# A two-layer transformer with experts: the small attention's end inside the next score loop, query/key products earlier between rows, other groups and another tail

## The reference

```python
x = _layernorm(x + _L0_attn_ref(x, ...))   # rms norm, 16 heads of 64, softmax over 256 keys
x = _layernorm(x + _L0_ffn_ref(x, ...))    # shared expert + 8 experts of 256, gates of the top 2
x = _layernorm(x + _L1_attn_ref(x, ...))   # per token: softmax over its own 16 heads of 8
x = _layernorm(x + _L1_ffn_ref(x, ...))    # 8 experts of 512, a token goes through its top 2
```

```python
scores = jnp.einsum('bnhd,bngd->bnhg', q, k) / SCALE
attn = jax.nn.softmax(scores, axis=-1)
out = jnp.einsum('bnhg,bngd->bnhd', attn, v)
```

## Time and profile before

| | us |
|---|---|
| median of 3 runs | 1618.16 (1617.31 to 1619.76) |
| the profiled execution | 1612.05 |
| its span, first to last instruction | 1610.3 |
| from the first to the last `OUT` residual (15 periods) | 1332.46 |
| behind the last `OUT` residual | 217.59 |
| granted TensorE clock, mean | 0.909 |

### The profile page before, as it was taken

How to read it: one execution, slowest core, us unless ns; L and a number is a source line. 1 busy time by engine, 2 the same in 40 slices (tenths; PEclk the granted TensorE clock), 3 DMA queues, 4 the chain that set the end, 5 groups by cost and what they waited for, 6 DMA issues and landing times. The chain is left out here.

```text
span 1610.3 us, 30931 instructions
## 1 busy us (share of the span) xinstructions
PE 1291.1 (80%) x10473; PEld 1110.6 (69%) x10473; DVE 983.1 (61%) x2660; ACT 776.3 (48%) x2206; POOL 626.6 (39%) x550
## 2 busy tenths in 40 slices
PE   6887878787888898898977888898888888876543
PEld 5776667675767787777766676786767676766533
DVE  4466666666566766767666655666775666644612
ACT  5664645455456555555544544465555444422110
POOL 3034352526162524243452624425163442533322
PEclk9998998898799999999998888999998899887756
DMA  7301211010021110201112120111032040115452
GB/s 245 122 2 51 78 44 60 1 50 1 11 89 60 50 57 20 79 14 41 60 54 68 54 65 12 59 49 40 23 115 89 11 133 12 63 41 185 141 165 64
DMA packets 79711, 103.76 MB, mean 64 GB/s; under 512 B 10042, under 2 KB 46531, under 8 KB 79555
## 3 DMA queue, kind: packets, MB, share of 16 engines
q1 hardware_dynamic: 75458, 93.38, 17.5%
...
...
## 5 line engine op out<-in xcount | busy, mean ns | idle before, releaser
L805 ACT ACTIVATE probs<-bank_S,neg_max 128x256 f32<-128x256 f32 x512 | 236.3, 477 | 227.8 <-DVE neg_max L922 204.7
L922 DVE TENSOR_REDUCE neg_max<-bank_S 128x2 f32<-128x512 f32 x256 | 164.7, 685 | 85.3 <-PE bank_S L1378 79.8
L683 POOL TENSOR_TENSOR hid<-hid,qkv 128x1024 f32<-128x1024 f32 x62 | 174.3, 2812 | 32.7 <-ACT hid L821 32.6
L1484 PE MATMUL bank_F<-down,hid 128*128 128x128 f32 x1024 | 136.6, 293 | 39.3 <-DVE x L1004 24.8
L638 POOL TENSOR_TENSOR var_eps<-mv,ln_eps 128x2 f32<-128x2 f32 x64 | 12.7, 198 | 398.0 <-DVE mv L960 397.9
L698 POOL DMA_INDIRECT xs<-x,slots_of x64 | 63.4, 990 | 257.7 <-DVE slots_of L1109 243.1
L1484 PEld LDWEIGHTS bank_F<-down,hid 128*128 128x128 f32 x1024 | 128.8, 206 | 46.2 <-DVE x L1004 29.4
L784 ACT ACTIVATE probsT<-bank_T 128x512 f32<-128x512 f32 x256 | 142.0, 609 | 34.4 <-PE bank_T L1407 31.8
L1407 PE MATMUL bank_T<-ident,probs 128*128 128x128 f32 x1024 | 150.8, 293 | 0.2 <-ACT probs L805 0.2
L671 POOL TENSOR_TENSOR hid<-qkv 128x1024 f32<-128x1024 f32 x47 | 115.6, 2460 | 76.0 <-ACT qkv L784 76.0
L1407 PEld LDWEIGHTS bank_T<-ident,probs 128*128 128x128 f32 x1024 | 122.2, 151 | 31.4 <-issue 29.3
...
## 6 DMA issues: line engine op xcount, KB each, us to landing
...
```

Of the source, the lines that this page charges most:

```text
L683: ins = g.tensor_tensor(pv1[:, t, half(i)], *weights_and_values(t, i), ALU.mult)
L805: ins = sc.activation(probs[:, h // 2 % 2, h % 2, t, :], unit.bank(f"S{h}")[:, t * S:(t + 1) * S], ACT.Exp, bias=neg_max[:, h, t:t + 1], a ...
L922: ve.tensor_reduce(neg_max[:, h, :], v.bank(f"S{h}")[:, :].rearrange("p (t k) -> p t k", t=NT), AX.X, ALU.max, negate=True).then_inc(max_r ...
L1484: ins = te.matmul(bank[:, (j * NT + t) * P:(j * NT + t + 1) * P], hid0[:, e, k, tokens(t)], down0[:, e, k, :], start=k == 0, stop=k == M0 - 1)
```

## The change

The arithmetic stays the same; order, buffers and grouping change.

- **The small attention's end.** `AOT`, `PROJ`, `X3T` and `R1` leave the seam. They stand in the score loop of the next iteration: `AOT` at step 0, `PROJ` at step 1, `X3T` and `R1` at step 4, `RK` at (5, 1), that is behind `T10` and `T11` and ahead of the scores `S14` and `S15`. `route(1)` (now `second_route`) runs on DVE in step 5 behind `head_scores(0)`, `place_row` in step 6, `gate` and `gate_row` in step 7, `map_blocks` behind that. `scatter` stands behind `value_product(0)` on POOL.
- **The seam.** `QK0` and `QK1` come ahead of `X1T`, `S0` and `S1` behind `U0_3`. DVE's `first_pair(0)` comes ahead of `ln_apply(0)`, `first_pair(1)` behind `X1T`, the first maxima behind `route(0)`. A wave that opens a group stands at the seam's end, other waves partly ahead of `X1T`.
- **Buffers.** `x3T`, `score1` and the second half of the products (`prod1`) get their own.
- **Groups.** Rows go in groups of 3, 4, 4, 4 and 1 in place of 4, 4, 4, 3 and 1. Waves have at most 6 blocks and begin at iterations 4, 8 and 12. Seven rows are gathered in the loop in place of eight; `combine` stands at step 3 and its norm at step 7. The last row's blocks are packed without gaps. The number of blocks, 99, stays.
- **The tail** has an order of its own (`tail_first`, `tail_second`): 12 blocks in iteration 16 and 22 in iteration 17, in place of 19 and 11.

```diff
-SLOTS = 8
+GROUPS = [range(0, 3), range(3, 7), range(7, 11), range(11, 15), range(15, 16)]
+COMPACT = len(GROUPS) - 1
+SLOTS = 6
 X3_ROWS = 10
...
-WAVE_SIZES = [(0, 5, [6, 6, 6, 5]), (1, 9, [6, 6, 6, 5]), (2, 13, [8, 8, 7])]
+WAVE_SIZES = [(0, 4, [5, 5, 5, 4]), (1, 8, [6, 6, 6, 5]), (2, 12, [6, 6, 6, 5])]
 WAVES = [(g, sum(sizes[:i]), n, first + i, first + i + 1) for g, first, sizes in WAVE_SIZES for i, n in enumerate(sizes)]
-WAVES += [(3, 0, 8, 16, 16), (3, 8, 8, 16, 16), (3, 16, 3, 16, 16), (4, 0, 8, 17, 17), (4, 8, 3, 17, 17)]
-
-GATHERS = {9: [0, 1], 10: [2, 3], 13: [4, 5], 14: [6, 7]}
+WAVES += [(3, 0, 6, 16, 16), (3, 6, 6, 16, 16), (3, 12, 6, 17, 17), (3, 18, 5, 17, 17), (4, 0, 6, 17, 17), (4, 6, 5, 17, 17)]
+
+GATHERS = {8: [0, 1], 9: [2], 12: [3, 4], 13: [5, 6]}
...
-FILL_B = {(0, 1): ["D0p2"], (1, 0): ["WT0"], (1, 1): ["D0p3"], (2, 0): ["D0base"], (3, 0): ["X2T"], (3, 1): ["LQ0", "LQ1"]}
-DOWN_PLACES = [(2, 1), (4, 1), (5, 1), (6, 1)]
+PLACES_B = {(0, 1): ["D0p2"], (1, 0): ["WT0"], (2, 0): ["D0p3", "D0base"], (3, 0): ["X2T"], (3, 1): ["LQ0", "LQ1"]}
+PLACES_C = {(0, 0): ["AOT"], (1, 1): ["PROJ"], (4, 0): ["X3T"], (4, 1): ["R1"], (5, 1): ["RK"]}
+DOWN_PLACES = [(2, 1), (4, 0), (5, 0), (6, 0)]
...
-        put("A", "X1T")
-        put("G", "U0_0", "U0_1")
-        put("A", "R0")
-        put("G", "U0_2", "U0_3")
-        put("G", "AOT", on=b)
-        put("G", "U0_4")
-        put("G", "PROJ", on=b)
-        put("A", "V3", on=nxt)
-        put("G", *blocks[2:3])
-        put("G", "X3T", on=b)
-        put("A", "QK0", "QK1", on=nxt)
-        put("G", *blocks[3:4])
-        put("G", "R1", on=b)
-        put("G", *blocks[4:5])
-        put("S0", "S0", on=nxt)
-        put("S1", "S1", on=nxt)
...
+    early, late = [], []
+    for w in waves_up(it):
+        (late if is_first(w) else early).append(w)
+    put("A", f"O{HP - 1}", "OUT")
+    put("F", *[name for w in early for name, _ in transpose_units(w)])
+    put("A", "V0", on=nxt)
+    put("G", "V1", on=nxt)
+    put("A", "V2", on=nxt)
+    put("A", "QK0", "QK1", on=nxt)
+    put("G", *[name for w in early for name in up_names(w)[:2]])
+    put("A", "X1T")
+    put("G", "U0_0", "U0_1")
+    put("A", "R0")
+    put("G", "U0_2", "U0_3")
+    put("S0", "S0", on=nxt)
+    put("S1", "S1", on=nxt)
+    put("G", "U0_4", "U0_5", "U0_6", "U0_7", "U0_8")
+    put("A", "V3", on=nxt)
+    put("G", *[name for w in early for name in up_names(w)[2:]])
+    put("G", *[name for w in late for name in [n for n, _ in transpose_units(w)] + up_names(w)])
...
-        aoT = x3T = x2T
+        aoT = x3T = sb("x3T", P, S)
+        prod1 = sb("prod1", P, E // NT, M0, S)
+        score1 = sb("score1", P, NT, NH1, NH1)
...
-                if v.c:
-                    scatter(v, v.it - 2)
+                if v.a and v.c:
+                    inverse_std(2, v.at(2, 1, 1))
+                if v.c and v.b:
+                    scatter(v, v.it - 2)
+                if v.b:
                     value_product(v, 1, (0,))
...
+                        blocks_out_at(v, 0)
+                        combine(GATHERS.get(v.it - 1, []))
+                    if s == 3 and v.next:
+                        input_norm(v)
+                    if s == 4:
+                        if v.c:
+                            transposed_out(v, "X3T", x3T)
+                            blocks_out_at(v, 1)
+                        if v.b:
+                            head_product(v)
+                    if s == 5:
+                        if v.b:
+                            head_scores(v, 0)
+                        if v.c:
+                            second_route(v)
+                            blocks_out_at(v, 2)
+                    if s == HP - 2:
+                        if v.next:
+                            input_transposed(v)
+                        if v.b:
+                            head_scores(v, 1)
+                        if v.c:
+                            place_row(v)
+                            blocks_out_at(v, 3)
+                    if s + 1 < HP:
                         inverse_sums(v, s + 1)
-                    if v.c and s == 1:
+                    if s == 2:
+                        if v.b:
+                            ln_apply(1, x2, v.at(1, 1, 1))
+                        if v.c:
+                            second_norm(v)
+                    if s == HP - 1 and v.c:
+                        combine_norm(GATHERS.get(v.it - 1, []))
                         gate(v, 1, 2)
                         gate_row(v)
...
+                if late:
+                    map_blocks(v)
                     head_softmax_sum(v, 0)
+                o_scale(v, HP - 1)
+                dve.wait_ge(xplus_ready, v.at(0, 1, 1))
+                residual(v, "OUT", x1, x_plus)
+                ln_stats(0, x1)
+                for w in early:
+                    blocks_transposed(v, w)
+                if v.next:
+                    first_pair(v, 0)
+                ln_apply(0, x1, v.at(0, 1, 1))
+                transposed_out(v, "X1T", halves=x1T)
+                if v.next:
+                    first_pair(v, 1)
+                    head_out(v, 0)
+                route(v, 0)
+                if v.next:
+                    head_max(v, 0)
+                    head_max(v, 1)
```

585 lines of the change are left out of this document (312 added, 273 removed).

## The result

The changed kernel takes **1708.49 us** (median of 4 runs, 1707.13 to 1709.67), the kernel before beside it 1618.96 (1617.31 to 1620.97): **1.0552 times** the time before, 95% interval 1.0534 to 1.0570. The forecast was 1714 (1610 to 1760, 0.75 for slower). The profiled execution spans 1707.6 us, 97.3 more than that of before; the forecast had 96. TensorE's mean granted clock fell from 0.909 to 0.881 of full speed.

What follows compares the result with a forecast made beforehand. The kernel was taken to be bound by a chain passing from engine to engine. 60.3 + 1424 (periods) + 222 (tail) = 1706 us of span, 96 over before; 1618 + 96 = 1714 us, range 1610 to 1760.

Steps and rivals of the forecast that it cites:

- Step 5: Late in the score loop, RK waits for the mask until 11.5 us; S14's maxima begin 15.4 us behind those before.
- The lock: In route(1) on DVE, the 4-column copy is held until POOL's value product ends: +3.0 us per loop.
- wide lock: Rival: the two small subtractions behind route(1)'s copy are held as well, +2.8 us in 14 iterations, 1753 us; chance 0.12.
- The slow clock: At the loop's end, PE idles ahead of RK, then runs at 1.2 GHz against 2.4: 3.4 us per iteration.
- Steps 6 and 7: Loop's end, from the maxima of S14 up to OUT, with other PE work behind slow scores: 16.9 us.
- Steps 0 to 4: Early score loop, with some DVE work leaving and other work coming in: 37.4 us against 36.5, bounds 34 to 39.
- The seam: The part of a row's period ahead of its loop, without the small attention's end: 20.5 us plain, against 28.9.
- Plain period: From one row's residual to the next, seam 20.5 plus loop 69.7: 90.2 us against 85.4.
- Waves, maps, gathers: Additions to the plain periods: 47 us for twelve iterations with waves, 10 for three maps, 35 for gathers.
- Sum of periods and tail: The fifteen row periods were put at 1424 us, what follows them at 222 us, bounds 210 to 245.
- Absorbed: Rival: moved DVE work falls into waits of the last two steps, PE stays fast; loop end 23, total 1584; chance 0.20.
- No lock: Rival: route(1)'s copy slips in ahead of POOL, −3.0 us in 14 iterations, 1672 us; chance 0.14.

Runs made afterwards that it cites:

- the filling: The changed kernel with 70 useless transposes of the identity on PE ahead of RK's wait for the mask; 1717.40 us, ratio 1.0646.
- the changed kernel's second trace: The changed kernel run again without an edit, beside the kernel before on the same chip; 1710.58 us, ratio 1.0591.

## Where the prediction was right, and where not

**Step 5 (15.4).** 15.07 to 15.88 in the loops of rows 2 to 4. The parts: `head_scores(0)` ended 7.1 us behind the maxima (6.4 forecast), the mask was there at 11.9 (11.5), `RK` took 2.2 (2.0), the scores 1.6 as forecast. The sum was right, with small errors in one direction. In rows 3 and 4 the subtraction of line 1084 takes 1.2 us and the step 15.9; in rows 6 to 8 it takes .42 and the step 15.07. Row 2 has the long subtraction and 15.07 too, since `RK` has six of its ten matmuls in a row that opens a group.

**The lock (3.0).** The copy took 2.66 us in place of .17 in 13 of the 14 loops and 2.31 in one: 2.5 held. Beside a gather it was .72. The other .55 came from the small subtraction, which met POOL's next instruction. Together 3.05. So the number was right and the account of it was not: both "lock" and "wide lock" are the same mechanism, which the reduction in place of the copy showed. As the rival "wide lock" was priced, at +2.8 on top, it would have had to meet the start of an instruction, and met the tail of a short one.

**The slow clock (3.4 per iteration).** Measured by its removal: 2.8, 3.1 and 2.5 in the three rows where the filling held the clock. `RK` and the scores make 1.6 of the 3.4 in the forecast's own numbers; the other 1.8, in steps 6 and 7, it doesn't work out (1.6 measured in rows 2 and 3). The transposes behind the wait were to show 1.95 as in the earlier trace rows; what stands there is `RK`, scores and a mixture, 1.92 us against 1.03 ahead of the wait; the transposes come last and took 1.37, the clock rising in them.

**Steps 6 and 7 (16.9).** 15.7 to 16.8 without a map but for the last (13.95); 16.3 in rows 2 and 3. `o_scale(7)` ended earlier than I had it (12.9 behind the maxima, not 14.4), and `OUT` came 3.4 us behind it in place of 2.44: its 32 products begin late, at 305.49, and take 4.86. Two errors that nearly cancel.

**Steps 0 to 4 (37.4).** 36.3 in row 3's loop (242.02 to 278.29). They were put at 0.9 above the 36.5 of before, and over the 14 loops they are 42 us shorter than before, most of it in the loops of rows 10, 11, 14 and 15, where they took 45 to 50 us and take 39 to 41 now.

**The seam (20.5) failed by 3 us.** It took 22.8 to 23.8 in plain rows. The step that failed is "between 0 and 3.5 more than row 0 paid, I take 1.6", and ahead of it row 0's own 16.9, which came to 18.9. PE waited 2.99 us ahead of `X1T`, and every product of the seam up to 328.1 ran at the lower level, the next row's scores among them:

```profile
317.10 0.41 PE L1473 MATMUL bank_A<-ident,x 128*128 128x128 f32 x2 [2.99 <-DVE x L1011]
...
325.29 0.58 PE L1503 MATMUL bank_S<-qk_hi,qk_lo 64*128 64x256 f32 x2
```

In row 5's seam, where a wave's products stand ahead of `X1T`, it is 22.33 at clock 1.00. A wave that stands there keeps PE at work through the wait, and the seam with it is no longer than the slow ones without. That the lower clock makes most of the 3 us is borne out by the changed kernel's second trace, where row 2's seam runs at 0.92 and takes 21.00, .5 over the forecast: the term between 0 and 3.5 was at its upper end and beyond here, and near 1.6 there. Since a wave keeps PE at work, 3.9 us per wave was too much.

**Plain period (90.2).** From row 1's residual to row 2's and from there to row 3's: 90.15 and 92.20, 91.2 on average.

**Waves, maps, gathers (92 in all).** 1418.7 less row 0's 68.7 and 14 × 91.2 leaves 73. Maps were mis-sized the other way: 3.4 each in the sum, some 7 at the loop's end (23.0 to 23.7 against 16.3), of which 2.7 to 3.2 is one held operation and the rest the map's other operations and what waits for them. So waves and gathers came to some 50 in place of 82; the gathers' waits in the seam were put at 4.5 each time, and by pairs of like rows with and without gathers they are .6 (rows 8 and 12 against 4), 0 (9 against 10) and 6.6 (13 against 14). The 6.6 isn't the gathers' own either: with the same gathers that seam takes 23.2 in the traces from chips of the other kind.

**Sum of periods and tail.** 1418.7 against 1424, 229.5 against 222. That the total came within 6 us rests on the end of the loop, which was worked out from rows, and on errors of 14 (periods), 12 (maps), −31 (waves and gathers) and 7 (tail) that went both ways: on luck as far as these cancel.

**The rivals.** "Absorbed" needed the routing off the path of the scores, and moving it there gave 1595. "No lock" and "clock up" were priced near what they cost (3.05 against 3.0, 2.5 to 3.1 against 3.4), though the first couldn't be had by itself: without the copy another operation is held. "The change doesn't do what it says" didn't come: in row 3's loop PE isn't idle ahead of `AOT`, and the waits nearest to `PROJ` and `R1` are 1.34 and .51 us. Of its signs, PE's wait ahead of `RK` was put at 6 to 9 us and is 7.1 to 9.6.
